# One written order for all 32 batches, banks named per batch, and two small operations moved

## The reference, cut to what matters

```python
# block 0 ("linear" attention, 8 heads of 32)
xn = ln(x); q = softmax(xn@Wq, over features of a head); k = softmax(xn@Wk, over tokens)
att = k^T v per head; y = q att; h = ln(y)*(1+scale)+shift; x = x + silu(h)@W_out
# block 1 (full attention, 16 heads of 16)
xn = ln(x); q, k, v = xn@Wq, xn@Wk, xn@Wv
att = softmax(q k^T); y = att v;  h = ln(y)*(1+scale)+shift; x = x + silu(h)@W_out
```

## Time and profile before

| | us |
|---|---|
| median of 3 runs | 959.7 (958.72 to 961.6) |
| profiled execution, its own time | 959.34 |
| its span | 957.5 |
| PE / DVE / ACT / POOL busy | 852.1 / 821.8 / 698.3 / 739.6 |
| mean granted TensorE clock | 0.953 |

### The profile page before, as it was taken

One profiled execution on the slowest core, in us unless ns is written; L12 is line 12 of the kernel. 1 busy time (PEld: TensorE's weight loads), 2 busy tenths in 40 slices (PEclk: granted clock), 3 DMA queues, 4 the chain that ended last, 5 costly groups with the idle time before them and its releaser, 6 DMA issues.

```text
span 957.5 us, 25672 instructions
## 1 busy us (share of the span) xinstructions
PE 852.1 (89%) x8715; PEld 614.1 (64%) x8715; DVE 821.8 (86%) x1678; ACT 698.3 (73%) x1236; POOL 739.6 (77%) x1212
## 2 busy tenths in 40 slices
PE   3866688899999999999999999999999998888774
PEld 1755576566777777777777777777777775554432
DVE  7869859899999999999999999999999998777732
ACT  0222364588888888888888888888888888778763
POOL 9345898788988888889888888888888877765221
PEclk9577899899999999999999999999999999999977
DMA  7111143434444544344434434343334332333100
GB/s 206 23 30 38 36 101 90 92 92 93 91 103 102 103 87 103 97 99 103 103 98 90 98 98 102 91 91 90 96 103 103 103 81 81 81 101 103 39 25 33
DMA packets 140090, 83.76 MB, mean 87 GB/s; under 512 B 78262, under 2 KB 132636, under 8 KB 139964
## 3 DMA queue, kind: packets, MB, share of 16 engines
q1 hardware_dynamic: 139964, 82.13, 35.7%
HBM read 39.52 MB, written 25.79 MB: 68 GB/s over the span
## 4 chain that ended last, share of the span: by engine, by line
DVE 38%; PE 33%; issue 17%; POOL 9%; ACT 1%; SPq 1%; DMA 1%; DVEq 0%; POOLq 0%; ACTq 0%
PE banks L696 10%; DVE NM L1061 10%; DVE st L962 6%; PE banks L683 4%; PE banks L664 4%; POOL XB L1777 4%; PE banks L607 3%; PE banks L541 3%; PE banks L618 3%; DVE wemb L1101 2%; DVE Y L1085 2%; DVE V L1003 2%; DVE V1t L1053 2%; DVE qm L992 2%; DVE km L976 2%
## 5 line engine op out<-in xcount | busy, mean ns | idle before, releaser
L1061 DVE TENSOR_REDUCE NM<-banks 128x4 f32<-128x1024 f32 x256 | 304.0, 1216 | 28.0 <-PE banks L664 25.4
L1582 ACT ACTIVATE wraw<-banks,uu 128x1024 f32<-128x1024 f32 x154 | 170.4, 1117 | 32.5 <-PE banks L683 31.7
L1754 POOL TENSOR_TENSOR SH<-ST,SH 128x512 f16<-128x512 f32 x64 | 84.5, 1320 | 52.5 <-ACT SH L1550 52.5
L1582 ACT ACTIVATE PX<-banks,uu 128x1024 f32<-128x1024 f32 x102 | 113.1, 1116 | 14.7 <-PE banks L683 14.2
L664 PE MATMUL banks<-SK,SQ 51*128 51x256 f16 x1024 | 100.5, 273 | 24.1 <-DVE V L1003 11.1
L541 PE MATMUL banks<-wo,SH 128*128 128x256 f16 x768 | 96.6, 284 | 14.5 <-POOL SH L1754 13.4
L683 PE MATMUL banks<-SQ,SK 53*128 53x256 f16 x1024 | 95.6, 274 | 6.2 <-DVE NM L1061 1.8
L541 PE MATMUL banks<-wv,ZT 128*128 128x256 f16 x768 | 98.5, 280 | 0.0
L1700 POOL TENSOR_TENSOR rs<-ve,nhalf 128x2 f32<-128x2 f32 x128 | 89.4, 698 | 10.6
L541 PEld LDWEIGHTS banks<-wo,SH 128*128 128x128 f16 x768 | 74.9, 101 | 33.0 <-POOL SH L1754 14.6
L696 PE MATMUL banks<-wraw,V 128*32 128x256 f32 x1232 | 88.6, 388 | 3.0 <-ACT wraw L1582 2.1
(11 more groups left out here) (186 smaller groups left out, 2012.8 us busy)
## 6 DMA issues: line engine op xcount, KB each, us to landing
scr<-AB SPq DMA_DIRECT2D x64, 256.0 KB, 3.0
X<-in_x_dram SPq DMA_DIRECT2D x32, 256.0 KB, 2.8
SK<-scr SPq DMA_DIRECT2D x64, 128.0 KB, 3.0
SQ<-scr SPq DMA_DIRECT2D x64, 128.0 KB, 2.7
out_dram<-wemb SPq DMA_DIRECT2D x32, 256.0 KB, 3.1
SK<-scr SPq DMA_DIRECT2D x64, 64.0 KB, 2.9
...
```

The source lines that it names most:

```text
L1061: V.tensor_reduce(NMe[:, c, :, 2 * g:2 * g + 2], banks[:, n:n + 2, :].rearrange("p a (h m) -> p a h m", m=T), AX.X, ALU.max, negate=True). ...
L1582: A.activation(px(v % 5), banks[:, n:n + 2, :].rearrange("p a n -> p (a n)"), ACT.Exp, scale=uu[:, 0:1]).then_inc(S["exp"])
L1754: G.tensor_tensor(SH[:, l, 1], ST[:, l], SH[:, l, 0], ALU.subtract).then_inc(S[f"sl{l}"])
```

## The change

What it does, part by part.

- **Order.** The loops with `at(...)` are gone. Each engine's program is a written list of calls for all 32 batches and the setup, as `k0(16); v0(16); q0(16); cols(8, 5); rows(10, 0)`. The order varies from batch to batch. It is drawn up once; at run time it is as fixed as before, and each engine still runs it in order.
- **Banks.** `BANK` names a bank for each step and batch (a string of 32 digits), and `FREED` names for each use the one or two last readers that `clear()` waits for.
- **Maxima.** `ntT` (two PE transposes per batch, one use of a bank) and `nt` (one DVE copy) go. A new SP step `nT` transposes NMw by DMA into NT, and `nw` waits for it.
- **Normalization.** `nm` goes; POOL's `norm` has two instructions, and the scaling steps subtract the mean straight from `mv`. `mv` and `rs` have two buffers, so that `s0` to `s3` wait for the scaling of the batch before the last one. `parts` (the one buffer Z) and `norm` wait for POOL's own earlier steps.
- **Setup.** The three first loads of x come ahead of the weights, and the setup steps stand elsewhere in the lists.

```diff
 BANK = {
-    "gk0": 3, "gkt": 3, "gq0": 2, ...
+    "gk0": "74522524141442153640733045072130",
 ...
-HELD = {
-    "gk0": ((("exp", 8, -59), ("max", 8, -50), ("max", 8, -51), ...
+FREED = {
+    "gk0": (
+        "- kt:1 fr2 kt:3 kt:4 Y0:4 max:3 ka:3 exp:2 exp:11 max:31 x1:8 exp:37 max:56 ka:10 qa:11 max:79 ka:13 "
 ...
+            def nT(b):
+
+                e.wait_ge(S["np"], b + 1)
+                if b >= 1:
+                    e.wait_ge(d_nw[(b - 1) % 2], 16 * ((b - 1) // 2 + 1))
+                e.dma_start(NT[:, :, :], NMw[:, :, :].rearrange("p c n -> p (c n)"), transpose=True).then_inc(d_nt[b % 2], 16)
+
             def nw(b):
                 o = b % 2
-                e.wait_ge(S["nt"], b + 1)
+                e.wait_ge(d_nt[o], 16 * (b // 2 + 1))
 ...
-                at(ty, i - 10, 0)
-                at(y1T, i - 11)
-                at(rows, i - 8, 4)
 ...
+            cols(8, 5); rows(10, 0); rows(10, 1); pv(8, 2); pv(8, 3); pv(8, 4); cols(8, 6); rows(10, 2); pv(8, 5)
+            cols(8, 7); y0(14); ktT(16); ty(8, 0); y1T(7); rows(10, 3); att(15); qtT(15); rows(10, 4); pv(8, 6)
 ...
-                G.tensor_scalar(nm[:, l, :], mv[:, l, :, 0], -1.0, 0.0, ALU.mult, ALU.add)
-                follow(G.tensor_scalar(ve[:, l, :], mv[:, l, :, 1], a, EPS * a, ALU.mult, ALU.add))
-                G.tensor_tensor(rs[:, l, :], ve[:, l, :], nhalf[:, :], ALU.pow).then_inc(S[f"r{l}"])
+                e.wait_ge(S[f"r{l}"], b)
+                follow(G.tensor_scalar(ve[:, l, :], mv[:, b % 2, l, :, 1], a, EPS * a, ALU.mult, ALU.add))
+                G.tensor_tensor(rs[:, b % 2, l, :], ve[:, l, :], nhalf[:, :], ALU.pow).then_inc(S[f"r{l}"])
```

More of the change, by code:

```diff
@@ new lines @@
+    "gty1": "25131111406600103101143212025031",
+    "gy1T": "07003515137314263145102030053400",
+    "go1": "51070445167232222142412040144210",
+    "gpm": "0",
+    "grow3": "1",
+    "gcnd": "4",
+    "gcol": "6",
+    "grow0": "0",
+    "gbb0": "0",
+    "grow1": "2",
+    "gbb1": "4",
+    "grow2": "5",
+    "gbb2": "4",
+    "gt_w0": "3",
+    "ga_w0": "3",
+    "gt_w1": "2",
+    "ga_w1": "7",
+    "gt_o0": "0",
+    "ga_o0": "0",
+    "gt_o1": "6",
+    "ga_o1": "6",
+    "gt_f0": "3",
@@ L158, in bass_cond_seq @@
         d_mk = [sem(f"d_mk{i}") for i in range(3)]
+        d_nt = [sem(f"d_nt{i}") for i in range(2)]
         d_nw = [sem(f"d_nw{i}") for i in range(2)]
@@ L645, in k1p @@
                     ready(e, "wl_k1")
-                feat_major(bank(BANK["gk1"]), ZT[:, b % 2, 1], W["k", 1]).then_inc(S["k1p"])
+                feat_major(bank(home("gk1", b)), ZT[:, b % 2, 1], W["k", 1]).then_inc(S["k1p"])
             def v1p(b):
@@ L666, in rows @@
                 m.then_inc(S["rows"])
-            def ntT(b):
-                e.wait_ge(S["np"], b + 1)
-                clear(e, "gnt", b)
-                nt = banks[:, BANK["gnt"], 0:P].bitcast(F16)
-                for c in range(2):
-                    m = PE.transpose(nt[:, c * P:(c + 1) * P], NMw[:, c, :], identb[:, :])
-                m.then_inc(S["ntT"])
             def cols(b, u):
-                g, c, r, n = u // 2, u % 2, b % 3, BANK[f"gc{u}"]
+                g, c, r, n = u // 2, u % 2, b % 3, home(f"gc{u}", b)
                 if u == 0:
@@ new lines, in _ @@
+            ar_f1(); o0(2); qtT(4); k0(5); v0(5); q0(5); y0(4); ktT(5); att(5); y0T(3); q1p(1); k1p(1); qtT(5)
+            v1p(1); rows(0, 0); rows(0, 1); rows(0, 2); y0(5); rows(0, 3); rows(0, 4); k0(6); v0(6); q0(6)
+            rows(0, 5); rows(0, 6); ktT(6); o0(3); q1p(2); rows(0, 7); k1p(2); y0T(4); att(6); v1p(2); qtT(6)
+            k0(7); v0(7); q0(7); y0(6); rows(1, 0); rows(1, 1); ktT(7); o0(4); att(7); rows(1, 2); rows(1, 3)
+            y0T(5); q1p(3); rows(1, 4); k1p(3); rows(1, 5); v1p(3); cols(0, 0); cols(0, 1); cols(0, 2); qtT(7)
@@ new lines, in _ @@
+            rows(1, 6); pv(0, 0); pv(0, 1); rows(1, 7); cols(0, 3); k0(8); cols(0, 4); cols(0, 5); cols(0, 6)
+            v0(8); q0(8); rows(2, 0); rows(2, 1); ktT(8); pv(0, 2); pv(0, 3); pv(0, 4); pv(0, 5); rows(2, 2)
+            cols(0, 7); ty(0, 0); rows(2, 3); pv(0, 6); pv(0, 7); rows(2, 4); rows(2, 5); rows(2, 6); ty(0, 1)
+            q1p(4); rows(2, 7); k1p(4); cols(1, 0); o0(5); cols(1, 1); qtT(8); cols(1, 2); cols(1, 3); pv(1, 0)
+            pv(1, 1); cols(1, 4); y0T(6); k0(9); v0(9); cols(1, 5); cols(1, 6); q0(9); pv(1, 2); pv(1, 3)
@@ new lines, in _ @@
+            o0(8); rows(5, 5); pv(4, 0); pv(4, 1); rows(5, 6); cols(4, 3); q1p(7); o1(2); cols(4, 4); rows(5, 7)
+            k1p(7); qtT(11); y0T(9); k0(12); v0(12); q0(12); cols(4, 5); rows(6, 0); pv(4, 2); rows(6, 1)
+            pv(4, 3); cols(4, 6); pv(4, 4); pv(4, 5); rows(6, 2); cols(4, 7); ty(4, 0); y0(10); ktT(12); att(11)
+            y1T(3); rows(6, 3); rows(6, 4); pv(4, 6); pv(4, 7); cols(5, 0); cols(5, 1); v1p(7); ty(4, 1)
+            cols(5, 2); pv(5, 0); pv(5, 1); rows(6, 5); cols(5, 3); rows(6, 6); q1p(8); o1(3); cols(5, 4)
@@ new lines, in _ @@
+            rows(6, 7); k1p(8); o0(9); qtT(12); y0T(10); k0(13); q0(13); cols(5, 5); cols(5, 6); pv(5, 2)
+            pv(5, 3); rows(7, 0); v0(13); rows(7, 1); rows(7, 2); cols(5, 7); pv(5, 4); pv(5, 5); ktT(13); y0(11)
+            ty(5, 0); y1T(4); rows(7, 3); rows(7, 4); att(12); pv(5, 6); pv(5, 7); cols(6, 0); cols(6, 1); v1p(8)
+            ty(5, 1); cols(6, 2); rows(7, 5); pv(6, 0); pv(6, 1); q1p(9); cols(6, 3); rows(7, 6); o1(4)
+            cols(6, 4); k1p(9); rows(7, 7); o0(10); y0T(11); qtT(13); k0(14); v0(14); q0(14); cols(6, 5)
@@ new lines, in _ @@
+            rows(8, 0); pv(6, 2); rows(8, 1); pv(6, 3); cols(6, 6); rows(8, 2); pv(6, 4); pv(6, 5); cols(6, 7)
+            ktT(14); ty(6, 0); y0(12); y1T(5); rows(8, 3); rows(8, 4); att(13); pv(6, 6); pv(6, 7); cols(7, 0)
+            cols(7, 1); v1p(9); ty(6, 1); cols(7, 2); rows(8, 5); pv(7, 0); pv(7, 1); cols(7, 3); rows(8, 6)
+            q1p(10); o1(5); k1p(10); o0(11); rows(8, 7); cols(7, 4); qtT(14); y0T(12); k0(15); v0(15); q0(15)
+            cols(7, 5); rows(9, 0); rows(9, 1); pv(7, 2); pv(7, 3); pv(7, 4); pv(7, 5); cols(7, 6); rows(9, 2)
@@ new lines, in _ @@
+            pv(8, 7); rows(10, 5); v1p(11); cols(9, 0); cols(9, 1); ty(8, 1); cols(9, 2); q1p(12); pv(9, 0)
+            pv(9, 1); cols(9, 3); rows(10, 6); k1p(12); o1(7); y0T(14); cols(9, 4); rows(10, 7); o0(13); qtT(16)
+            k0(17); v0(17); q0(17); cols(9, 5); rows(11, 0); pv(9, 2); rows(11, 1); pv(9, 3); cols(9, 6)
+            rows(11, 2); pv(9, 4); pv(9, 5); y0(15); ktT(17); ty(9, 0); rows(11, 3); cols(9, 7); y1T(8); att(16)
+            rows(11, 4); cols(10, 0); pv(9, 6); pv(9, 7); cols(10, 1); v1p(12); ty(9, 1); rows(11, 5); cols(10, 2)
@@ new lines, in _ @@
+            rows(11, 6); pv(10, 0); pv(10, 1); q1p(13); cols(10, 3); rows(11, 7); o1(8); k1p(13); cols(10, 4)
+            o0(14); y0T(15); qtT(17); k0(18); v0(18); q0(18); cols(10, 5); rows(12, 0); rows(12, 1); pv(10, 2)
+            pv(10, 3); cols(10, 6); rows(12, 2); pv(10, 4); pv(10, 5); cols(10, 7); ktT(18); y0(16); ty(10, 0)
+            cols(11, 0); cols(11, 1); y1T(9); rows(12, 3); att(17); q1p(14); cols(11, 2); rows(12, 4); pv(10, 6)
+            pv(10, 7); pv(11, 0); pv(11, 1); rows(12, 5); v1p(13); ty(10, 1); cols(11, 3); rows(12, 6)
@@ new lines, in _ @@
+            cols(11, 4); k1p(14); o1(9); rows(12, 7); k0(19); o0(15); qtT(18); y0T(16); v0(19); q0(19)
+            cols(11, 5); cols(11, 6); pv(11, 2); pv(11, 3); rows(13, 0); rows(13, 1); pv(11, 4); pv(11, 5)
+            cols(11, 7); rows(13, 2); ty(11, 0); ktT(19); y0(17); y1T(10); rows(13, 3); att(18); rows(13, 4)
+            pv(11, 6); pv(11, 7); cols(12, 0); v1p(14); cols(12, 1); ty(11, 1); cols(12, 2); rows(13, 5)
+            pv(12, 0); pv(12, 1); cols(12, 3); rows(13, 6); q1p(15); o1(10); k1p(15); cols(12, 4); rows(13, 7)
@@ new lines, in _ @@
+            pv(14, 4); pv(14, 5); cols(14, 7); ktT(22); ty(14, 0); y1T(13); rows(16, 3); att(21); y0(20)
+            cols(15, 0); cols(15, 1); pv(14, 6); pv(14, 7); rows(16, 4); cols(15, 2); pv(15, 0); pv(15, 1)
+            ty(14, 1); v1p(17); rows(16, 5); cols(15, 3); rows(16, 6); q1p(18); o0(19); o1(13); cols(15, 4)
+            rows(16, 7); k1p(18); qtT(22); y0T(20); k0(23); q0(23); cols(15, 5); rows(17, 0); pv(15, 2); pv(15, 3)
+            v0(23); rows(17, 1); cols(15, 6); rows(17, 2); pv(15, 4); pv(15, 5); ktT(23); cols(15, 7); y0(21)
@@ new lines, in _ @@
+            ty(15, 0); y1T(14); att(22); rows(17, 3); rows(17, 4); pv(15, 6); pv(15, 7); cols(16, 0); v1p(18)
+            cols(16, 1); ty(15, 1); cols(16, 2); rows(17, 5); pv(16, 0); pv(16, 1); rows(17, 6); cols(16, 3)
+            q1p(19); o0(20); o1(14); cols(16, 4); rows(17, 7); k1p(19); qtT(23); y0T(21); k0(24); v0(24); q0(24)
+            cols(16, 5); rows(18, 0); pv(16, 2); rows(18, 1); pv(16, 3); ktT(24); cols(16, 6); rows(18, 2)
+            pv(16, 4); pv(16, 5); cols(16, 7); y0(22); ty(16, 0); y1T(15); rows(18, 3); att(23); cols(17, 0)
@@ new lines, in _ @@
```

(40 more changed lines are left out.)

843 lines of the change are left out of this document (422 added, 421 removed), and 190 rows, old and new, of tables (BANK, FREED, HELD).

## The result

The changed kernel takes 1031.15 us (median of 4 runs, 1027.65 to 1034.73), against 959.7 for the kernel before: ratio 1.0742, 95% interval 1.0701 to 1.0783. The profiled execution has a span of 1032.9 us, 75.4 more than the 957.5 of before. I had forecast 925 us, and slower with a chance of 0.08: the forecast was wrong in its sign.

The account below looks back on a forecast made before the run. PE was taken to bound the full pipeline, no engine the filling. Gains of 1 + 13 + 3 + 5 + 11 + 1 = 34 us gave 957.5 - 34 + 1.8 = 925.3, forecast as 925 us, range 902 to 951.

Parts of the forecast that it names:

- (d): POOL's normalization: dropping nm removes 25.8 us of POOL, hidden in the pipeline, at most 6 us in filling, counted there.
- (e): Maxima by DMA transpose nT on SP: landing taken as 3.1 us, 1.9 us spare, nothing either way if SP is free.
- a stall of SP: Rival, chance 0.07: nT's wait for np_ holds SP's later transfers, so rows and k0 come late each period; 980 us.
- (a): ntT gone from PE: 0.11 us to the next start, 32 of them 3.5 us of PE.
- (b): PE's lists change more often between kinds of matmul: 0.11 us per change, 32 more, 3.5 us more of PE.
- (c): nt gone from DVE: 8.6 us of DVE, taken as 0 on the path, at most 3 us.
- The order: Written lists recover half the busiest engine's idle time in filling, pipeline and draining; with the ends, 34 us.
- Start: 0 to 43 us: r0(0) could start 3 us sooner, but k0(0) needs the split weights; 1 us gained.
- Filling: 43 to 215 us: half of DVE's idle time of 26.35 and 6.8 us, 13 + 3 = 16 us gained.
- The middle: 3 us for the rest of filling (147 to 215 us) and 5 us for the full pipeline.
- Draining: 766 to 912 us: half of PE's 21.6 us idle time, 11 us gained.
- Lock-up of DVE by POOL: Rival, chance 0.15: packed filling puts DVE beside POOL, whose holds lengthen DVE's small steps and cancel filling's gain; 943 us.

Follow-up runs that it names:

- e1: The changed kernel with the old normalization (nm written again, scaling steps add and multiply), all else as changed: 927.74 us, ratio to before 0.9655.
- e5: The kernel before with the DMA transpose nT in place of ntT and nt: 960.38 us, ratio 1.0007.
- e6: e1 with the four memsets of SQ and SK made by ACT instead of POOL: 921.37 us, ratio to before 0.9594.
- e3: The kernel before with nm as the positive mean, subtracted in the scaling steps, waits and buffers as before: 1061.94 us, one run.
- e4: The changed kernel with add in place of subtract in the scaling steps, which changes the result: 920.36 us, one run.

## Why the prediction was wrong, step by step

**The step that failed is (d).** It said that the new normalization removes 25.8 us of POOL's work and that nothing of it costs. I priced what the diff removed and took the duration of the scaling steps from before, because their shape, type, engine and count stayed. Their pair of operations did not: (add, mult) became (subtract, mult). By the runs, 256 instructions went from 0.56 to 1.25 us, 179 us more of POOL. The scale of the harm could have been read from the rows that I had: POOL was busy for 486.6 of 551 us, so 64/22 = 2.9 us of a period were free, and the new form adds 8 x 0.7 - 0.8 = 4.8. But no row of before held a (subtract, mult) on POOL; its `tensor_scalar` rows there are all of quick pairs, (add, mult), (mult, add) and (mult, mult). I took the new form for one of them without a reason, where for `nT` in (e) I had taken bounds from the nearest rows. None of my rivals had it, and my range ended at 951. Even a bound from the nearest row, POOL's two-tile operation on 128x256 elements (681 ns in the lines view of before), would have given only 0.12 x 256 = 32 us of POOL, which the spare time covers; the true price lay outside what the trace of before could tell. The slower rival that I had, a stall of SP, did not occur: in e1, where `nT` and its place in the lists are as in the change, the period is 25.07 us. Its price was also wrong by its own terms: 3 us on 29 batches are 87 us, which gives 1012 and not 980.

**Steps (a), (b), (c), (e)**: I had net zero on the path. For (a), (c) and (e) e5 measures 0.7 us, with an interval around none. PE's busy time fell by 9.3 us where I had 3.5 for `ntT`: the pair is busy for 0.28 us, 9.0 us in 32 batches, and I had counted only the 0.11 us to the next start. It made no difference. (b) has no run of its own; its 0.11 us comes from a place where the type changes too, from f16 to f32, and no run tells the two apart.

**The order**, which I summed to 34 us, gave 32.1 in e1's span. By the table above, with e1's two rows:

```profile
L1159 DVE TENSOR_REDUCE km<-banks x32: 657/678/983, 55.9 to 748.6; 128x2 f32<-128x512 f32 x32
...
L1244 DVE TENSOR_REDUCE NM<-banks x256: 1159/1214/1225, 132.8 to 881.1; 128x4 f32<-128x1024 f32 x128
```

- Start: -1 forecast, +10.7 measured. POOL's memsets do end sooner, at 26.7 us and not at 28.4. But the new lists put the mask's casts on DVE beside POOL's memsets, ahead of what PE waits for, and `v0(0)` and `q0(0)` ahead of `k0(0)`.
- Filling, to the first `max_`: -13 forecast, -25.5 measured. POOL's wait for `mv` in 43 to 147 us went from 33.6 us to 15.1, below the 20 that I had set.
- The middle: -8 forecast (3 for the rest of filling, 147 to 215 us, and 5 for the pipeline), -4.4 measured. The period did not shorten: 25.07 us in e1 against 25.03. So the gain is in the uneven periods at its two ends, and my 4.5 us from PE's 0.41 us of idle per period was wrong. e1's window from its eleventh `k0` to its last:

```profile
221.80:748.30 526.50, 515.46 (x5552) 370.14 (x5550) 491.52 (x959) 440.37 (x793) 463.09 (x774) 1.00 0.40 100
```

PE is busy for 97.9% of it, and was for 98.3% before; e5 shows the same from the other side.
- Draining: -11 forecast, -11.9 measured. The tail: -1 and -1.0.

That the sum agrees to 2 us rests on errors of opposite sign: 11.7 us in the setup and 3.6 in the middle against 12.5 in filling and 0.9 in draining. The setup and filling hang together, as e6 shows. Without the memsets beside DVE its first `km` starts 7.2 us sooner than before, and filling gains 12.6 us (89.8 against 102.4), next to the 13 that I had. e1 starts 17.9 us later than e6 and is 5.0 us behind it at the first `max_`: filling won back 12.9 us of the late start. The half of the idle time was a choice, and that it came out so near is in part luck. e6's two rows:

```profile
L1159 DVE TENSOR_REDUCE km<-banks x32: 656/678/981, 38.0 to 742.9; 128x2 f32<-128x512 f32 x32
...
L1244 DVE TENSOR_REDUCE NM<-banks x256: 1159/1214/1226, 127.8 to 876.3; 128x4 f32<-128x1024 f32 x128
```

**Lock-up of DVE by POOL.** That `km`'s small operation is held by POOL was right, and the trace of before could have shown it. From its timeline, one with POOL idle and one beside POOL's work:

```profile
45.94 0.23 DVE L977 TENSOR_SCALAR km<-km,un 128x2 f32<-128x2 f32 x1
...
392.65 1.16 POOL L1782 TENSOR_TENSOR AB<-R,AB 128x512 f16<-128x512 f32 x1
392.97 0.87 DVE L977 TENSOR_SCALAR km<-km,un 128x2 f32<-128x2 f32 x1
```

The long one ends at 393.84 us, POOL's instruction at 393.81. Of the 32, 28 took 0.41 to 0.92 us, and each of them ended within 0.03 us behind a POOL instruction that had begun before it. What the rival made of it went the other way: in e1 the median is 229 ns against 862 before, with 10 of the 32 held, so the lists took most of these holds away. The period didn't shorten by that. In the setup the lock was there and cost more than I had thought, as e6 shows.

The changed kernel's other signs fit this reading. Its first `max_` is at 141.0 us, outside my 128 to 138, and e1's at 132.8 inside it; the period of 28.6 is over my 25.1, and the one engine that I said one should then look for is POOL, by its work and not by a gap. In e1 the last `k0`, at 748.3, and the wait for `mv` are as I had them, and the period of 25.07 us is not.

What stays open: why the new form costs 14 us more in the new lists (103) than in the loops (89), where lists drawn up for one set of durations then meet another (the subtraction alone, with `nm` kept or left out on both sides, is 102 us in the loops by e3 and 111 in the lists by e4, one run each); and which steps of PE and DVE together set the period of 25.03 us, which neither e5's lighter PE nor the new lists shortened.
